# Cross attention with a low-rank context: zero products ahead, a split product turned round, low products last and x group 3 moved in the queues

## The reference, cut to what matters

```python
# x: (16, 100, 640), ctx_768: (16, 722, 384), HEADS = 8, NUM_TOKENS = 4
enc, ca = ctx[:, :718], ctx[:, 718:]                     # 718 keys, 4 "low" context rows
query, keyt, valt = x @ Wq, enc @ Wk, enc @ Wv
hs = _mha(query, keyt, valt)                             # 8 heads of 80, softmax over 718 keys
ca_q1 = jnp.einsum('btc,th->bch', ca, Wq_ca)[:, indices, :]
ca_hs1 = _mha(ca_q1, x, x)                               # 100 x 100 per head
ca_q2, ca_k2, ca_v2 = ca_hs1 @ Wq, ca @ Wk_ca, ca @ Wv_ca
ca_hs2 = _mha(ca_q2, ca_k2, ca_v2)                       # 4 keys per head
out = (hs + ca_hs2) @ Wout + b_out + x
```

## Time and profile before

| | |
|---|---|
| median of 3 runs | 1041.4 us (1039.96 to 1042.91) |
| the profiled execution's own time | 1037.99 us |
| its span, first to last instruction | 1036.3 us |
| PE busy | 996.6 us, 96% of the span |
| DVE, ACT, POOL busy | 62%, 47%, 33% |
| mean granted TensorE clock | 0.987 |

### The profile page before, as it was taken

One profiled execution on the slowest core, in us unless ns is written; L12 is line 12 of the kernel. 1 busy time (PEld: TensorE's weight loads), 2 busy tenths in 40 slices (PEclk: granted clock), 3 DMA queues, 4 the chain that ended last, 5 costly groups with the idle time before them and its releaser, 6 DMA issues.

```text
span 1036.3 us, 20985 instructions
## 1 busy us (share of the span) xinstructions
PE 996.6 (96%) x6876; PEld 975.5 (94%) x6876; DVE 644.1 (62%) x1122; ACT 485.3 (47%) x893; POOL 346.6 (33%) x289
## 2 busy tenths in 40 slices
PE   7997989999999999999999999999999999998998
PEld 7986989999999999999999999999999999998997
DVE  5523666666666666666666767676666666665444
ACT  6333444545454636453536364635454545454110
POOL 5142252515161616051524243324333333433000
PEclk9988999999999999999999999999999999998999
DMA  7978767697969796968687878788787878785354
GB/s 253 256 260 245 203 182 190 162 193 168 185 169 188 174 184 172 187 165 186 170 192 172 177 183 173 191 163 204 155 203 156 205 147 197 164 189 151 96 175 152
DMA packets 154171, 190.12 MB, mean 183 GB/s; under 512 B 80930, under 2 KB 108194, under 8 KB 154146
## 3 DMA queue, kind: packets, MB, share of 16 engines
q1 hardware_dynamic: 150096, 181.23, 74.0%
q10 hardware_dynamic: 4048, 8.56, 2.6%
HBM read 81.56 MB, written 19.95 MB: 98 GB/s over the span
## 4 chain that ended last, share of the span: by engine, by line
PE 70%; DMA 7%; SPq 7%; DVE 6%; ACT 6%; issue 4%; POOL 0%; ACTq 0%; DVEq 0%; POOLq 0%
PE psB L796 22%; PE psS L761 19%; PE psS L900 5%; PE psS L736 4%; PE psT L777 4%; PE psT L819 4%; SPq L375 4%; DMA encT_raw<-in_encT_dram 3%; PE psT L825 2%; SPq L372 2%; PE psB L935 2%; DMA enc_raw<-in_encN_dram 2%; DVE negmax L1456 1%; PE psS L947 1%; ACT encN_h L1149 1%
## 5 line engine op out<-in xcount | busy, mean ns | idle before, releaser
L761 PE MATMUL psS<-encT_keep,Wk_keep 128*128 128x360 f32 x1440 | 255.4, 331 | 2.6 <-POOL encT_keep L645 2.6
L761 PEld LDWEIGHTS psS<-encT_keep,Wk_keep 128*128 128x128 f32 x1440 | 239.7, 190 | 3.0 <-issue 2.9
L796 PE MATMUL psB<-PT_h,encN_h 120*128 120x400 f32 x576 | 204.3, 355 | 4.9 <-DVE UT L1485 2.4
L796 PE MATMUL psB<-PT_l,encN_h 120*128 120x400 f32 x576 | 200.0, 347 | 0.0
L796 PE MATMUL psB<-PT_h,encN_l 120*128 120x400 f32 x576 | 199.9, 347 | 0.0
L1112 ACT ACTIVATE probs<-psS,negmax 100x718 f32<-100x718 f32 x128 | 110.3, 861 | 140.0 <-DVE negmax L1456 139.8
L615 POOL TENSOR_TENSOR encT_keep<-encT_raw,encT_keep 128x718 fp32r<-128x718 f32 x45 | 79.8, 1773 | 185.6 <-ACT encT_keep L1142 181.0
L606 POOL TENSOR_TENSOR Mbd<-Mbd,fmask 128x320 fp32r<-128x320 f32 x48 | 47.9, 998 | 250.2 <-DMA Mbd<-m_split 247.7
L1480 DVE TENSOR_TENSOR kT<-psS,kT 128x718 fp32r<-128x718 f32 x80 | 72.4, 905 | 91.6 <-ACT kT L1137 91.3
L1137 ACT ACTIVATE kT<-psS 128x718 fp32r<-128x718 f32 x80 | 61.7, 771 | 124.1 <-PE psS L761 120.5
L796 PEld LDWEIGHTS psB<-PT_h,encN_h 120*128 120x128 f32 x576 | 109.6, 190 | 6.2 <-DVE UT L1485 3.1
(11 more groups left out here) (219 smaller groups left out, 1650.1 us busy)
## 6 DMA issues: line engine op xcount, KB each, us to landing
kstack<-kT SPq DMA_DIRECT2D x64, 448.8 KB
kstack<-kT SPq DMA_DIRECT2D x192, 112.2 KB
enc_raw<-in_encN_dram SPq DMA_DIRECT2D x48, 360.0 KB, 5.2
encT_raw<-in_encT_dram SPq DMA_DIRECT2D x45, 359.0 KB, 6.1
kstack<-kT SPq DMA_DIRECT2D x32, 359.0 KB
kstack<-kT SPq DMA_DIRECT2D x32, 269.2 KB
kstack<-kT SPq DMA_DIRECT2D x32, 179.5 KB, 3.1
kstack<-kT SPq DMA_DIRECT2D x64, 89.8 KB, 3.2
```

The source lines that it names most:

```text
L761: mm = pe.matmul(keys_in(f, first)[:, half, 0:HALF], w[:, c, f * 128:(f + 1) * 128], e[:, c, k0:k0 + HALF], start=(j == 0), stop=(j == 3 * ...
L796: mm = pe.matmul(psB[:, 1, 0:RH], e[:, k, c * 128:(c + 1) * 128], a[:, k, half * RH:(half + 1) * RH], start=(j == 0), stop=(j == 3 * KT - 1))
```

## The change

1. **Zeros first.** DVE clears `st2` and half of `gbd`, and PE multiplies these zeros 12 times (128x400 into psB) ahead of `first_queries`. In `first_queries` the first piece goes high by high for all five outputs, then with the low part of x, then with that of Wq. x group 0, piece 0, is rounded by DVE, not ACT. Three of the five x loads go from ACT's queue to SP's, between the Wq loads.
2. **Small keys turned round.** `ca_keys` makes rows of k2 (context stationary, 320 columns of weights moving): 12 matmuls where there were 72, then `turn_ca_keys`, 8 transposes, with two copies ahead and an addition behind. v2 goes to psS[1] and waits for four `q_low`.
3. **Order of stage 1.** `query(1, h)` is ahead of `m_head(h)` and `query(2, 0)` ahead of `m_head(6)`; `enc0_low` goes from POOL to DVE; `xT_high(3, c)` go from behind `k_high(0, 2)` to between `m_high` and `k_high(0, 1)`, and `load_xT(3)` from behind two lifts to ahead of `store_m`.
4. **Low products last.** `context` does the 12 matmuls with the context's high part first and the 6 with its low part last, and waits for the low parts only there, part by part.
5. **x M stationary.** In `b2_scores2` XM (64 columns) is stationary and both parts of P1T move (200 columns): 8 matmuls where there were 16. The result lies turned, is copied by DVE (`c2_copy`), turned back by PE (`b2_turn_parts`, 2 transposes), and added up by one reduction.
6. **Order of a batch.** `b2_scores2` goes ahead of `scores(i, 7)`; on ACT `pt_high(i, 3)` goes ahead of `enc_high(i, 0)`, `xm_high` ahead of `expo(i, 6)`, `enc_high(i, 2)` behind `hs_copy`; in batch 15 `context(15, 0)` takes the place where other batches have `keys`, and `high`/`low` of the first output tile come behind `u_high(15, 1)` and `pt_high(15, 6)`.

```diff
 # PE, context
-                        pe.wait_ge(s["encN"], PARTS * (i + 1))
+                        pe.wait_ge(s["encNhi"], PARTS * (i + 1))
...
-                    for k in range(KT):
-                        for e, a in products(eN, PT):
-                            mm = pe.matmul(psB[:, 1, 0:RH], e[:, k, c * 128:(c + 1) * 128],
-                                           a[:, k, half * RH:(half + 1) * RH], start=(j == 0), stop=(j == 3 * KT - 1))
+                    for k in range(KT):
+                        for p in range(2):
+                            pe.matmul(psB[:, 1, 0:RH], eN[0][:, k, cc], PT[p][:, k, rows],
+                                      start=(k == 0 and p == 0), stop=False)
+                    for k in range(KT):
+                        if u == 0 and k % KQ == 0:
+                            pe.wait_ge(s["encN"], PARTS * i + k // KQ + 1)
+                        mm = pe.matmul(psB[:, 1, 0:RH], eN[1][:, k, cc], PT[0][:, k, rows],
+                                       start=False, stop=(k == KT - 1))
 # PE, b2_scores2
-                    for h in range(HEADS - 1):
-                        high(h)
                     for h in range(HEADS):
-                        pe.matmul(psB[0:S, 0, 0:HT], P1T[1][:, h, :], XM[:, h, 0:HT], start=False, stop=False)
-                    high(HEADS - 1).then_inc(s["b2c"], 1)
+                        mm = pe.matmul(psB[0:2 * HT, 0, 0:2 * S], XM[:, h, :], P1T_both[:, h, :],
+                                       start=(h == 0), stop=(h == HEADS - 1))
+                    mm.then_inc(s["b2c"], 1)
+
+                def b2_turn_parts(i):
+                    pe.transpose(psB[0:S, 0, 0:2 * HT], c2_parts[:, 0:S], ident[0:2 * HT, 0:2 * HT])
+                    pe.transpose(psB[0:S, 0, 2 * HT:3 * HT], c2_parts[0:HT, S:2 * S], ident[0:HT, 0:HT])\
+                      .then_inc(s["b2t2"], 1)
 # PE, batch
-                    if last:
-                        values(i - 1, 1)
                     scores(i, 6)
-                    if not first and not last:
+                    if not first:
                         values(i - 1, 1)
                     if last:
-                        b2_scores2(i)
+                        context(i, 0)
                     else:
                         keys(i + 1, 0)
                     turn(i, 4, first)
+                    b2_scores2(i)
                     scores(i, 7)
-                    context(i, 0, first)
+                    if not last:
+                        context(i, 0, first)
+                    pe.wait_ge(s["c2copy"], i + 1)
                     turn(i, 5)
+                    b2_turn_parts(i)
 # PE, program
+                pe.wait_ge(s["warm"], 2)
+                warm = gbd[:, 0:4, :].rearrange("p h j -> p (h j)")
+                for n in range(12):
+                    pe.matmul(psB[:, 1, 0:RH], warm[:, 0:128], warm, start=True, stop=True)
                 first_queries()
                 ca_keys()
                 ca_values()
+                turn_ca_keys()
                 for h in range(HEADS):
-                    m_head(h)
                     if h < NP:
                         query(1, h)
-                query(2, 0)
+                    if h == NP:
+                        query(2, 0)
+                    m_head(h)
 # PE, ca_values
                     pe.wait_ge(s["wlo"], 4)
+                    pe.wait_ge(s["qlo"], 4)
 # SP
                 store_g(1)
+                load_xT(3)
                 for c in range(FT):
                     store_m(c)
...
                 lift(0, 1, first=True)
-                load_xT(3)
 # DVE
+                def c2_copy(i):
+                    dve.wait_ge(s["b2c"], i + 1)
+                    nc.vector.tensor_copy(c2_parts, psB[0:2 * HT, 0, 0:2 * S]).then_inc(s["c2copy"], 1)
...
-                        low(0, 0)
                         u_low(i, 1)
...
                     pt_low(i, 6)
                     if last:
+                        low(0, 0)
                         low(0, 1)
```

251 lines of the change are left out of this document (145 added, 106 removed).

## The result

The changed kernel takes 1033.0 us (median of 4 runs, 1031.99 to 1034.32), beside 1040.7 for the kernel before in the same measurement (4 runs, 1039.96 to 1042.91): a ratio of 0.9919, 95% interval 0.9896 to 0.9941. It is faster, by 7.7 us or 0.8%; the forecast was 31.2, and 1033.0 lies outside its range. The profiled execution has a span of 1030.3 us, where it was 1036.3.

A forecast was written before the change was run, and what follows sets the result against it. PE, busy for 96% of the 1036.3 us span, was taken as the bound. Terms 15.4 + 3.5 + 12.8 - 0.5 = 31.2 us off a 1041.4 us median gave 1010 us, range 1003 to 1021.

The forecast's parts named there:

- The loop, wait: Wait of values for pt_low in each loop batch: 0.65 of 0.78 us go, 14 x 0.65 = 9.1 us.
- The loop, b2_scores2: Fewer matmuls in b2_scores2, less two added transposes: 0.45 us a batch saved, 6.3 us in the loop.
- The longer chain: Low context's added round trip between PE and DVE: taken 0, bound 0.5 us a batch lost; as a rival 1017, chance 0.10.
- The loop, sum: All loop gains together: 9.1 + 6.3 = 15.4 us, at worst 6, at best 19.
- Start of stage 1: Zero products and small keys gain time at the start, but 0 us counted, as the first context's load covers it.
- 63 to 80 us: From keys(0, 0), starting near 63 instead of 69.95, to keys(0, 2): gain 3.5 us, bounds 1 and 6.
- 80 us to the loop: Batch 0's PE waits and slow-clock stretches go: 14.3 us, less 1.5 for SP, DMA and norm: 12.8, bounds 7 and 14.3.
- My rival of SP and the DMA engines: They take back the gain of stage 1 and batch 0, leaving 6 of 16.3 us: 1020.5 us, chance 0.17.
- Batch 15: Last batch: old waits shrink, new ones before context(15, 0) and the first tile; -0.5 us, bounds -2 and +2.

The follow-up runs named there:

- e2: Changed kernel with hs_copy(i - 1, 1) ahead of expo(i, 6) on ACT and hs_add ahead of xm_low on DVE; median 1029.3 us, ratio 0.9867.
- e8: Changed kernel with POOL's first low part of the context held until DVE's norm(i, 5) is done; median 1029.4 us, ratio 0.9910.
- e1: Changed kernel with the two new transposes made over all 100 rows instead of 64 and 32; median 1031.8 us, ratio 0.9899.
- e15: The changed kernel itself, unaltered, profiled and timed again; median 1032.5 us, ratio 0.9902.
- e12: Changed kernel plus e1, e2, e8, e9, a reordered last batch, and batch 0's b2_exp2 ahead of wv_high(0); median 1025.2 us, ratio 0.9872.
- e11: Changed kernel without its 12 products of zeros at the start; median 1027.4 us, ratio 0.9872.
- e5: Kernel before with only the change's batch edits, stage 1 left as it was; median 1030.0 us, ratio 0.9908.
- e9: Changed kernel with x group 3's five loads behind all stores of M, and batch 1's context loads behind the first lifts; median 1028.3 us, ratio 0.9898.

## Why the prediction failed, step by step

- **The loop, wait** (0.65 us a batch). Right: from `turn(3)` to `values` it is 3.00 us before, 2.33 now, 0.67 less. The batch shown had a wait of 0.78 where an undisturbed one has 0.72, so between undisturbed batches it is 0.61. "Cover of 2 us and more. Cost taken: 0" for the moved `enc_high` was wrong: it let POOL start beside `norm(i, 5)`, which cost 0.12 to 0.13 a batch at `turn(4)` (shown by e2 and e8) and part of the wait in batch 15 (e8).
- **The loop, b2_scores2** (0.45). The eight matmuls take 0.80 (forecast 0.82). The two transposes were priced as "0.077 each, so 0.15" by a row of 100 x 100 ones, and take 0.50: 0.35 a batch or 4.9 us missing. That puts the term below its worse bound of 0.29. e1 shows that the shape, not their number, costs it. The longer chain cost nothing, as taken.
- **The loop, sum**: from `turn(3)` to `turn(4)` 0.61 - 0.12 = 0.49 less (8.25 before, 7.76 now), from `turn(4)` to `turn(6)` 0.16 less (9.42 before, 9.26 now). That is 0.65 instead of 1.10 a batch between undisturbed batches, and 0.63 with landings counted (0.47 in e15). Of 15.4 came 8.8 (6.6 in e15). In e12, whose batches are shorter, landings took the further gain back, so a batch at my 15.4 would probably have met the same.
- **Start of stage 1** (0). Right (e11): `ca_values` waits, `keys(0, 0)` at 63.8.
- **63 to 80 us** (3.5). `keys(0, 0)` right; I had `k_high(0, 0)` at 77.7 and it came at 80.1, as I had counted the five loads' issues (the first store of M is issued 2.1 us later) and not their bytes ahead of it, which make its landing 2.1 us longer. PE waited 1.9 us at `keys(0, 1)`, which I had not seen, and `keys(0, 2)` started at 81.9, 1.1 us of gain. The clock fell behind it (mean granted clock 0.64 from 82.0 to 86.7 us, 18 matmuls in 4.79 us).
- **80 us to the loop** (12.8). This step failed most. The waits it named did go, but it treated them as losses that come back when removed, with 1.5 us taken off for SP and the DMA engines. `k_high(0, 2)` waited 7.18 us for the lift, the first scores came 3.3 us later than before, and new waits of PE (1.9, 2.6, 1.7, 3.2 us), each with a fall of the clock behind it in the first profile, took the place of the old ones: PE was idle for 13.9 us between 62 us and batch 1, and for 12.5 before. The bound from 7 was too high: of 16.3 us up to batch 1 came 0.7 in one profile and 3.3 in the other. e5 came there 1.8 us sooner than before with no edit of stage 1 at all. My rival of SP and the DMA engines, at 0.17, named it and was itself too mild: it left 6.
- **Batch 15** (-0.5). The waits were 3.0 and 2.3 us as I had worked them out (2.8 and 2.4), but I took the same tile start as a full account. Counted from the first turn, the first tile started 0.6 us later (36.1 against 35.5) and its 30 matmuls ran 1.5 us slower at the lower clock (5.9 against 4.3). PE then waited 1.75 us before a later tile, where it had waited 0.41, as its input came 1.3 us later behind the issue of the loads. Within rounding these make the 3.5 us lost; in e15 it was 5.1.

So the mechanisms were mostly named; the error was in the sum. It gave each removed wait its full price and took only 1.5 us off for the next resource in line: the chain of stores and lifts over SP and the DMA engines. The range had the same fault: the worse bounds of the terms add up to 6 + 1 + 7 - 2 = 12 us, a time of 1029, but the range ended at 1021; the measured gain of 7.7 lies beyond even that sum. What stays open is why the 3 to 4 us that e9 wins back at the lift and the first scores don't show at the loop (169.8, and 169.9 in e15), and what decides in an execution whether the clock falls behind a wait.

## What to carry to other kernels

When waits of one engine are removed, walk the slowest other chain (here issue, bytes ahead, landing, ring) to the same point before adding up: the gain ends where that chain ends. Before a wait is priced with a fall of the clock, look at a second profile: the fall may not be there. Price a new instruction by a row of its own shape, or pad it to a shape that the rows show. A split copy that is moved also moves the GpSimd work behind it, and that can land beside a VectorE instruction, which here took 2.19 us instead of 0.60.

## What the runs showed of the hardware that I had not expected

- Two transposes over 64 and 32 rows behind ones over 100 took 0.50 us, and 0.17 when padded to 100 rows (e1), with the matmul behind them of 128 rows in both.
- A TENSOR_SCALAR on 100 x 718 took 2.19 us beside a GpSimd subtraction and 0.60 alone (e8), while `pt_low`, which reads PSUM, took its 0.78 us beside one too (508.44 in the kernel before, where the GpSimd part ran from 507.99 to 509.81).
- A store issued into a queue behind five loads of 1 MB together landed after 4.8 us, and after 3.0 (e9) or 2.7 (the kernel before) without them; the stores behind it ran at their old pace (8.7 us from its landing to the last one's split in both).
- Behind the same wait of 1.7 us the granted clock was 0.57 in one execution and 1.00 in another of the same kernel.
